# Attention on one core: prologue and first step in one order, first keys in two loads, next operands on GpSimd's queue

## The chip, the cores and the metric

The kernel runs on one core of one Trainium2 chip. The metric is the device time of the whole program in microseconds. Before the change it is 2620.65 us, the median of 3 runs (2619.8 to 2622.64). The engines are PE (TensorE, matmuls), DVE (VectorE), ACT (ScalarE), POOL (GpSimd) and SP (SyncE, which only issues DMAs here). All times in the traces count from the start of the program's first instruction.

## What is computed

The reference is two layers on 2 x 2048 tokens of width 256. The first is a linear recurrence beside a sign-weight projection. The second, to which this case belongs, is an attention with linear position biases, beside a block with its own attention and a mixture of eight experts. The two attentions of the second layer are computed by one function of the kernel:

```python
# first attention: 16 heads of 16, biases by distance
scores = einsum('bhqd,bhkd->bhqk', Q, K) / sqrt(hd) + slopes[:, None, None] * rel
attn   = softmax(where(rel <= 0, scores, -inf))
out    = einsum('bhqk,bhkd->bqhd', attn, V)
# second attention: 16 query heads on 4 key heads, rotary positions, causal
scores = einsum('bqhd,bkhd->bhqk', apply_rope(q), apply_rope(k)) * scale
probs  = softmax(where(causal, scores, min))
attn   = einsum('bhqk,bkhd->bqhd', probs, v)
```

## The kernel before

The program runs in stages: front, middle, attention, after, experts. The change is in the attention (`attention`, from line 974) and in the functions that make its order (from line 896).

The attention has 16 steps (`STEPS`). A step is one batch and a group of four heads; steps 0 to 7 are the first attention, 8 to 15 the second. A step has five kinds of work:

- **max**: the scores of 128 queries against up to 512 keys for two heads, two matmuls that use one half of the array's rows each (line 1214), with masks on the diagonal (four short matmuls, line 1203). DVE reduces each of the two results to row maxima (line 1410). A step has 80 such pairs: 8 of query block 0, 16 of block 1, 24 of block 2, 32 of block 3.
- **rows**: when a block of 512 queries has all its maxima, DVE joins them (line 1417), POOL splits them into a high and a low part (`parts`, lines 1166 and 1168), PE transposes these (line 1241), ACT copies the rows out (line 1356), and SP stores them into two rows of the query operand (line 1105), so that the next matmul subtracts the maximum. 4 a step.
- **score**: the transposed scores of 128 keys against 512 queries for two heads (line 1229), and two exponentials on ACT (line 1366). 80 pairs a step.
- **value**: the product of four heads' exponentials with the values (line 1329), a group of 8 matmuls in the trace. 40 a step.
- **turn**: the output of a query block, copied by ACT (line 1390), turned by PE (line 1338), divided by DVE (lines 1437 and 1441) and stored by SP (line 1135). 4 a step.

The order of this work is written out by hand: the string `ORDER` has one letter for each (m, r, s, v, t), and every engine goes through it and takes its own share. A step's string begins at max 50 (`LEAD`), rows 3 (`AHEAD`) and score 5 (`SLEAD`): it does the last 30 maxima of its own step and the first 50 of the next. Results of max, score, rows and turn go into a ring of seven PSUM banks (`RING`); `slot_table` gives each its place, and `free_slots` lets PE wait until the bank's last user is done.

Before step 0 stands a prologue of its own on each engine. `orders` builds its list, `BEFORE`: the 50 maxima, with a rows five maxima behind the last one of its block, then the 5 scores. PE waits for all of the step's keys (`s_k`, line 1281) before the first max of block 1; until then it reads 512 keys from `k0a`, which an earlier stage has written. At its end PE waits for all of its maxima, rows and exponentials (lines 1289 to 1291).

The DMA queues: SP loads all keys of step 0 (lines 1110 to 1118, six DMAs of 256 KB and two of 96 KB), its values (line 1119), then stores the prologue's three rows, and then loads the operands of step 1 (lines 1122 and 1123; nine pieces in `LOADS`, two DMAs each but for the last). POOL loads the operands of step t + 2 during step t (line 1183), and puts fills of zeros for a later stage between them (line 1157).

Of the kernel before, what the change touches and what calls it, by code (L numbers as in the profile page):

```python
# [8 lines left out]
F32 = mybir.dt.float32  # L9
# [4 lines left out]
P = 128  # L14
B, L, D = 2, 2048, 256
# [910 lines left out]
NGR = NSP // PAIRS  # L926
LAST_MAX = [max(m for m in range(NMX) if MAXES[m][0] == qb) for qb in range(NQB)]
# [9 lines left out]

def orders():

    kinds = {"m": "max", "r": "rows", "s": "score", "v": "value", "t": "turn"}
    count = {"m": LEAD, "r": AHEAD, "s": SLEAD, "v": 0, "t": 0}
    work = []
    for k in ORDER:
        work.append((kinds[k], count[k]))
        count[k] += 1  # L950
    first = []
    for m in range(LEAD):
        first.append(("max", m))
        first += [("rows", qb) for qb in range(AHEAD) if min(LAST_MAX[qb] + 5, LEAD - 1) == m]
    first += [("score", s) for s in range(SLEAD)]
    whole = {"max": NMX, "rows": NQB, "score": NSP, "value": NGR, "turn": NQB}
    last = [(what, k) for what, k in work if k < whole[what]]
    return first, work, last
# [15 lines left out]
def attention(nc, A, M):  # L974
# [4 lines left out]
    with ExitStack() as ctx:  # L979
# [25 lines left out]
        s_k = sem("att_first_keys_loaded")  # L1005
# [18 lines left out]
        BEFORE, WORK, LAST = orders()  # L1024
        HELD = slot_table(WORK)[1]
        HELD += [("pad", 0)] * (-len(HELD) % RING)
# [17 lines left out]
        def work_of(t):  # L1044
            return LAST if t == STEPS - 1 else WORK
# [48 lines left out]

        block = ctx.enter_context(nc.Block())

        @block.sync
        def _(sp):
# [11 lines left out]
            for j in range(2):  # L1110
                for n in range(NPROD):
                    at = HALF * j + n * HD
                    sp.dma_start(k_op[0][at:at + HD, :, :].bitcast(F32),
                                 M["ka_d"][PROD_K[n], 0:GH * HD, :].rearrange(
                                     "(p j d) t -> j d p t", p=PAIRS, j=2)[j]).then_inc(s_k, 16)
                at = HALF * j + DOTS
                sp.dma_start(k_op[0][at:at + SLOPED + 2, :, :].bitcast(F32),
                             M["aug_d"][SLOPED:2 * SLOPED + 2, j * PAIRS:(j + 1) * PAIRS, :]).then_inc(s_k, 16)
            load(sp, 0, ("values", 0, 0))
            for n in range(AHEAD):  # L1120
                rows(0, n)
            for piece in LOADS:
                load(sp, 1, piece)
# [20 lines left out]
        def _(pool):  # L1144
# [25 lines left out]
            for n in range(AHEAD):  # L1170
                parts(0, n)
            for i in range(STEPS * FILLS, HSROWS // P // FILL):
                empty_rows(i)

            def step(t):
                for what, n in work_of(t):
                    if what == "rows":
                        parts(t, n)
                    elif what == "score" and (n - SLEAD) % LOAD_EVERY == 1 and (
# [12 lines left out]
        def _(pe):  # L1192
# [14 lines left out]
            def max_pair(r, n, outs, keys=None):  # L1207
# [4 lines left out]
                for j in range(2):  # L1212
                    part = slice(HALF * j, HALF * j + max_row(r))
                    ins = pe.matmul(outs[j][:, 0:w], q_op[o][part, p, qt * P:(qt + 1) * P],  # L1214
                                    (keys or k_op[o])[part, kp, k0:k0 + w], start=True, stop=not diagonal)
# [5 lines left out]
            def score_pair(r, n, outs):  # L1221
# [5 lines left out]
                for j in range(2):  # L1227
                    part = slice(HALF * j, HALF * j + max_row(r) + 2)
                    ins = pe.matmul(outs[j][:, c0:QB], k_op[o][part, kp, kt * P:(kt + 1) * P],  # L1229
# [14 lines left out]
            def free_slots(t, held, first, count):  # L1244

                last = {}
                for u in range(first - RING, first - RING + count):
                    past = u < 0
                    what, n = HELD[u] if past else held[u]
                    while what == "pad":  # L1250
                        u -= RING
                        what, n = HELD[u]
# [12 lines left out]
            first_at, first_held = slot_table(BEFORE)  # L1265
            for what, n in BEFORE:
                u = first_at[what, n]
                past = first_held[max(0, u - RING):max(0, u - RING + (1 if what == "rows" else 2))]
                done = [k + 1 + MD0 for kind, k in past if kind == "max"]
                taken = [k + 1 + RE0 for kind, k in past if kind == "rows"]  # L1270
                if done:
                    pe.wait_ge(s_md, max(done))
                if taken:
                    pe.wait_ge(s_re, max(taken))
                exped = [k + 1 + EX0 for kind, k in past if kind == "score"]
                if exped:
                    pe.wait_ge(s_ex, max(exped))
                if what == "max":
                    if n == LAST_MAX[0] + 1:

                        pe.wait_ge(s_k, (2 * NPROD + 2) * 16)
                    max_pair(0, n, [ps[(u + j) % RING] for j in range(2)], M["k0a"] if n <= LAST_MAX[0] else None)
                elif what == "score":
                    if n == 0:
                        pe.wait_ge(s_mr[0], NMR)
                    score_pair(0, n, [ps[(u + j) % RING] for j in range(2)])
                else:
                    turn_rows(0, n, u % RING)
            pe.wait_ge(s_md, 2 * LEAD + MD0)
            pe.wait_ge(s_re, AHEAD + RE0)  # L1290
            pe.wait_ge(s_ex, 2 * SLEAD + EX0)

            def step(t):
# [3 lines left out]
                for what, n in work:  # L1297
# [3 lines left out]
                    if what == "max":  # L1301
                        if n == NMX:
# [968 lines left out]
```

## Time and profile before

| | us |
|---|---|
| median of 3 runs | 2620.65 (2619.8 to 2622.64) |
| profiled execution | 2615.48 |
| its span, first to last instruction | 2613.6 |
| busy in the span: PE, DVE, ACT, POOL | 2339.5, 1918.1, 1515.9, 577.7 |

The span is what the profile sees of the profiled execution; the rest of its time lies around it. Busy times are of the whole program, which goes through stages with different limits, so that they say little about one of them. The attention is the middle part, from some 383 us on to 2010 us. Its stretches are read from views that are cut by time.

### The profile page before, as it was taken

Reading aid. Unit: us, or ns where it says so; the run is one execution under the profiler, and the core shown is the slowest. Engines: PE = TensorE matmul, PEld = TensorE weight load, DVE = VectorE, ACT = ScalarE, POOL = GpSimd, SP = SyncE. Lnnn points to the kernel's source line nnn. Section 1 sums busy time; section 2 is a strip of 40 time slices with the busy share of each in tenths; the row PEclk is TensorE's granted clock in tenths of the full one; section 3 lists DMA queues with packets and bytes.
Section 4 is the critical chain, followed back from the end, with each engine's and each line's share of the span. In section 5 each row is a group of like instructions: output and inputs, shape, how many; then the busy total and the mean of one; then the engine's idle time right before and its main releaser. Section 6 shows DMA issues by size and latency. Waiting matters only on the chain. (4 is left out here: it accounts for less than half of the span.)

```text
span 2613.6 us, 52877 instructions
## 1 busy us (share of the span) xinstructions
PE 2339.5 (90%) x18274; PEld 1272.9 (49%) x18275; DVE 1918.1 (73%) x4030; ACT 1515.9 (58%) x3290; POOL 577.7 (22%) x836
## 2 busy tenths in 40 slices
PE   3299986999999999999999999999997882899997
PEld 2155542444444444444444444444442652788886
DVE  6767666899999999999999999999991563233332
ACT  2033321787787787787787787777776551222221
POOL 4412100111111111111111111111000265523323
PEclk9599995899999999999999999999998995999999
DMA  4157673933433433322322322322102884344443
GB/s 153 60 169 213 203 198 54 134 74 74 79 75 72 81 75 71 68 53 48 68 53 48 69 53 47 69 53 46 33 30 87 280 271 166 78 76 77 76 77 69
DMA packets 169670, 246.99 MB, mean 94 GB/s; under 512 B 52196, under 2 KB 127092, under 8 KB 163408
## 3 DMA queue, kind: packets, MB, share of 16 engines
q0 software_dynamic: 37328, 107.98, 22.2%
q1 hardware_dynamic: 127136, 127.58, 17.6%
q10 hardware_dynamic: 4992, 8.55, 0.9%
q8 instruction: 138, 2.26, 0.4%
q14 instruction: 76, 0.62, 0.1%
HBM read 120.63 MB, written 122.36 MB: 93 GB/s over the span
## 5 line engine op out<-in xcount | busy, mean ns | idle before, releaser
L1410 DVE TENSOR_REDUCE a_mx<-banks 128x1 f32<-128x512 f32 (+3 forms) x2560 | 1379.8, 604 | 150.0 <-PE banks L1214 78.8
L1366 ACT ACTIVATE a_p<-banks 128x512 f32<-128x512 f32 (+3 forms) x2560 | 1177.3, 541 | 317.7 <-PE banks L1229 196.5
L1329 PE MATMUL banks<-a_p,a_v 128*32 128x512 f32 (+3 forms) x5120 | 599.8, 543 | 1.0 <-ACT a_p L1366 0.6
L1214 PE MATMUL banks<-a_k,a_q 48*128 48x512 f32 (+7 forms) x1600 | 340.3, 428 | 8.7 <-DVE a_mx L1410 1.9
L1229 PE MATMUL banks<-a_q,a_k 50*128 50x512 f32 (+7 forms) x1600 | 332.2, 426 | 11.3 <-ACT a_p L1366 4.6
L1214 PEld LDWEIGHTS banks<-a_k,a_q 52*128 52x128 f32 (+1 forms) x1600 | 155.0, 184 | 207.3 <-DVE a_mx L1410 165.9
L1229 PEld LDWEIGHTS banks<-a_q,a_k 54*128 54x128 f32 (+1 forms) x1600 | 152.4, 184 | 199.9 <-DVE a_mx L1410 144.9
L1214 PE MATMUL banks<-a_k,q 52*128 52x512 f32 (+7 forms) x944 | 215.3, 459 | 27.2 <-DMA a_k<-aug_rows 14.2
L1229 PE MATMUL banks<-q,a_k 54*128 54x512 f32 (+3 forms) x960 | 202.1, 434 | 10.4 <-ACT a_p L1366 6.0
L2048 ACT ACTIVATE e_hT<-banks 128x256 fp32r<-128x256 f32 x72 | 27.6, 383 | 311.6 <-PE banks L1976 311.6
L1989 PE MATMUL banks<-w,e_hT 128*128 x576 | 184.5, 422 | 9.4 <-DVE e_hT L2088 9.4
L1214 PEld LDWEIGHTS banks<-a_k,q 48*128 48x128 f32 (+1 forms) x944 | 96.6, 196 | 146.7 <-DVE a_mx L1410 109.1
L1950 POOL DMA_INDIRECT out_rows<-e_y,e_token x72 | 111.5, 1549 | 254.2 <-DVE e_y L2108 165.9
L2088 DVE TENSOR_TENSOR e_hT<-banks,e_hT 128x256 fp32r<-128x256 f32 x72 | 30.6, 424 | 174.7 <-ACT e_hT L2048 174.7
L1329 PEld LDWEIGHTS banks<-a_p,a_v 128*32 128x32 f32 x5120 | 102.9, 108 | 113.4 <-issue 64.1
L1229 PEld LDWEIGHTS banks<-q,a_k 54*128 54x128 f32 (+1 forms) x960 | 92.4, 188 | 132.8 <-DVE a_mx L1410 79.9
L2008 PE MATMUL banks<-w,e_gT 128*128 x576 | 136.6, 380 | 1.4 <-DVE e_y L2108 1.1
L1989 PEld LDWEIGHTS banks<-w,e_hT 128*128 128x128 f32 x576 | 110.1, 192 | 33.6 <-issue 10.7
L1203 PE MATMUL banks<-fill,before 64*128 64x64 bf16 x2048 | 125.9, 199 | 0.0
L1203 PE MATMUL banks<-fill,after 64*128 64x64 bf16 x2048 | 121.9, 197 | 0.0
L2008 PEld LDWEIGHTS banks<-w,e_gT 128*128 128x128 f32 x576 | 104.0, 191 | 13.3 <-issue 2.3
L1157 POOL DMA_DIRECT2D expert_rows<-a_zeros x132 | 98.8, 748 | 2.8 <-issue 2.8
(257 smaller groups left out, 2465.9 us busy)
## 6 DMA issues: line engine op xcount, KB each, us to landing
expert_rows<-a_zeros POOLq DMA_DIRECT2D x132, 258.0 KB, 5.4
e_x<-expert_rows SPq DMA_DIRECT2D x72, 129.0 KB, 3.0
a_k<-ka_parts POOLq DMA_DIRECT2D x36, 256.0 KB, 6.4
expert_rows<-e_y SPq DMA_DIRECT2D x72, 128.0 KB, 2.2
qa_parts<-m_part SPq DMA_DIRECT2D x16, 512.0 KB, 4.7
ka_parts<-m_part SPq DMA_DIRECT2D x16, 512.0 KB, 5.1
va_tiles<-m_va SPq DMA_DIRECT2D x8, 1024.0 KB, 5.3
qb_parts<-m_part SPq DMA_DIRECT2D x16, 512.0 KB, 4.7
```

The source lines that it names most:

```text
L1157: pool.dma_start(hs[:, i * FILL:(i + 1) * FILL, :], zeros[:, :, :]).then_inc(s_zs, 16)
L1203: ins = pe.matmul(outs[j][:, HALF * n:HALF * (n + 1)], steps[n][half, :], fill[half, :], start=False, stop=(n == 1))
L1214: ins = pe.matmul(outs[j][:, 0:w], q_op[o][part, p, qt * P:(qt + 1) * P], (keys or k_op[o])[part, kp, k0:k0 + w], start=True, stop=not dia ...
L1229: ins = pe.matmul(outs[j][:, c0:QB], k_op[o][part, kp, kt * P:(kt + 1) * P], q_op[o][part, p, qb * QB + c0:(qb + 1) * QB], start=True, sto ...
L1329: ins = pe.matmul(ps_o[VW * h:VW * h + VW, c0:QB], v_op[o][:, kt, hk * VW:hk * VW + VW], prob[:, (n * GH + h) % NPB, c0:QB], start=(kt == ...
L1366: nc.scalar.activation(prob[:, (2 * n + j) % NPB, c0:QB], ps[(slot + j) % RING][:, c0:QB], ACT.Exp, scale=SCALE).then_inc(s_ex, 1)
L1410: v.tensor_reduce(mx[:, j, p, qt, k0 // WIDE:k0 // WIDE + 1], ps[banks[j]][:, 0:w], AX.X, ALU.max).then_inc(s_md, 1)
L1950: pool.indirect_dma_start(out=out, out_offset=bass.IndirectOffsetOnAxis(ap=token[n % R][:, :], axis=0), in_=y[n % R][:, :], in_offset=None ...
L1989: ins = pe.matmul(bank[:, :], hT[c][s][:, k, :], of[:, ds(e * KD + k, 1), part * FFN:(part + 1) * FFN].rearrange("p o m -> p (o m)"), star ...
L2008: ins = pe.matmul(ps_y[:, 0:D], gT[s][:, f, :], w2[:, ds(e * FT + f, 1), :].rearrange("p o m -> p (o m)"), start=(f == 0), stop=(f == FT - 1))
L2048: nc.scalar.activation(hT[0][s][:, :, :].rearrange("p k t -> p (k t)"), ps_h[:, 0:D], ACT.Copy).then_inc(s_hi, 1)
L2088: v.tensor_tensor(hT[1][s][:, :, :].rearrange("p k t -> p (k t)"), ps_h[:, 0:D], high, ALU.subtract).then_inc(s_hT, 1)
```

## The change

The prologue and step 0 become one list. A new string, `FIRST_ORDER`, gives it entry by entry: 130 maxima (the 80 of step 0 and the first 50 of step 1), 85 scores, 40 value products, 7 rows and 4 turns. The loops over `BEFORE` on PE, ACT and DVE and PE's waits at the prologue's end are gone, and step 0 takes the new list (`work_of`). The first rows stands behind the eighth max. Keys below 512 are read from `k0a` throughout step 0 (`keys_of`), by the scores too.

The keys of step 0 from 512 to 1023 are loaded by SP, those from 1024 to 2047 by ACT, which loads the values behind them; each part has a semaphore, and PE waits for the first at max 9 and for the second at max 26 (`KEYED`). The operands of step 1 are issued by POOL, a piece at max 20, 25, ... 60, each when PE has scored that many; those of step 2 at score 26, 33, ... 82. Four fills of zeros move from before step 0 to the start of step 1.

```diff
+KEYED = [min(m for m in range(NMX) if MAXES[m][3] >= k0) for k0 in (WIDE, 2 * WIDE)]
...
+FIRST_ORDER = (
+    "mmmmmmmmrmmmmmmmmmsmmsmmsmsmmsvmmmmrvmmsmmmsmsmmsmvvsmmmvsmsmsmmvsmsmmmsvsmsmsvmsmrtsmms"
+    "vmmvsmmsvvmsmsmmsvsmsmmvsmsmvsmmsmsmvsmsmmsmvsmsmmssvmmsvmmsmsmmrmsmmvsmsvmmmsvmmvssmmvs"
+    "msvmmsmmvsmrmsmsvssmmvmsmmsvmsmsmvsmsmsmrvsmsmvsmsvmsmsvstsmsvmsmsmvsmsmvsssmmvsmsvvmsst"
+    "tr"
+)
...
+    first = numbered(FIRST_ORDER, {"m": 0, "r": 0, "s": 0, "v": 0, "t": 0})
+    work = numbered(ORDER, {"m": LEAD, "r": AHEAD, "s": SLEAD, "v": 0, "t": 0})
...
-            return LAST if t == STEPS - 1 else WORK
+            return FIRST if t == 0 else LAST if t == STEPS - 1 else WORK
...
+        def first_step_keys(eng, done, lo, hi):
+
+            for j in range(2):
+                for n in range(NPROD):
+                    at = HALF * j + n * HD
+                    eng.dma_start(k_op[0][at:at + HD, :, lo:hi].bitcast(F32),
+                                  M["ka_d"][PROD_K[n], 0:GH * HD, lo:hi].rearrange(
+                                      "(p j d) t -> j d p t", p=PAIRS, j=2)[j]).then_inc(done, 16)
...
-            load(sp, 0, ("values", 0, 0))
-            for n in range(AHEAD):
-                rows(0, n)
-            for piece in LOADS:
-                load(sp, 1, piece)
+            first_step_keys(sp, s_k[0], BT, 2 * BT)
...
-            for n in range(AHEAD):
-                parts(0, n)
-            for i in range(STEPS * FILLS, HSROWS // P // FILL):
-                empty_rows(i)
-
             def step(t):
+                if t == 1:
+                    for i in range(STEPS * FILLS, HSROWS // P // FILL):
+                        empty_rows(i)
                 for what, n in work_of(t):
                     if what == "rows":
                         parts(t, n)
-                    elif what == "score" and (n - SLEAD) % LOAD_EVERY == 1 and (
+                    elif t == 0 and what == "max" and n % 5 == 0 and 0 <= n // 5 - 4 < len(LOADS):
+                        pool.wait_ge(s_mt, n)
+                        load(pool, 1, LOADS[n // 5 - 4])
+                    elif t == 0 and what == "score" and n % 7 == 5 and 0 <= n // 7 - 3 < len(LOADS):
+                        pool.wait_ge(s_sc, n)
+                        load(pool, 2, LOADS[n // 7 - 3])
+                    elif t > 0 and what == "score" and (n - SLEAD) % LOAD_EVERY == 1 and (
...
-            for what, n in BEFORE:
...
-            pe.wait_ge(s_md, 2 * LEAD + MD0)
-            pe.wait_ge(s_re, AHEAD + RE0)
-            pe.wait_ge(s_ex, 2 * SLEAD + EX0)
...
+                        if t == 0 and n == KEYED[0]:
+                            pe.wait_ge(s_k[0], NFK)
+                        if t == 0 and n == KEYED[1]:
+                            pe.wait_ge(s_k[1], NFK)
...
+            first_step_keys(act, s_k[1], 2 * BT, L)
+            load(act, 0, ("values", 0, 0))
```

How the instructions stand: on PE, from the eighth max pair (512 keys from `k0a`) on. Before, the maxima of block 1 follow (keys `a_k`), and the transposes of the first rows (`a_mpart`) stand among them:

```order
L1214 MATMUL banks<-k0a,q 128x512 x2
L1203 MATMUL banks<-fill,before 128x64 x4
L1214 MATMUL banks<-a_k,q 128x512 x2
L1214 MATMUL banks<-a_k,q 128x128 x2
L1203 MATMUL banks<-fill,before 128x64 x4
L1214 MATMUL banks<-a_k,q 128x512 x2
L1214 MATMUL banks<-a_k,q 128x256 x2
L1203 MATMUL banks<-fill,before 128x64 x4
L1214 MATMUL banks<-a_k,q 128x512 x2
L1241 MATMUL banks<-ident,a_mpart 8x128 x4
```

After, from the same pair on (line 1235 is the max, 1262 the transposes):

```order
L1235 MATMUL banks<-k0a,q 128x512 x2
L1220 MATMUL banks<-fill,before 128x64 x4
L1262 MATMUL banks<-ident,a_mpart 8x128 x4
L1235 MATMUL banks<-k0a,q 128x512 x2
L1235 MATMUL banks<-a_k,q 128x128 x2
L1220 MATMUL banks<-fill,before 128x64 x4
L1235 MATMUL banks<-k0a,q 128x512 x2
L1235 MATMUL banks<-a_k,q 128x256 x2
L1220 MATMUL banks<-fill,before 128x64 x4
```

The transposes moved ahead of the maxima of block 1, and the first of these reads `k0a`.

Further on in the same list on PE, after: scores (line 1250) and a value product (1329) stand among the maxima of blocks 1 and 2, where before there were maxima and rows alone up to the fiftieth pair.

```order
L1235 MATMUL banks<-a_k,q 128x384 x2
L1220 MATMUL banks<-fill,before 128x64 x4
L1250 MATMUL banks<-q,k0a 128x384 x2
L1220 MATMUL banks<-fill,after 128x64 x4
L1235 MATMUL banks<-k0a,q 128x512 x2
L1235 MATMUL banks<-a_k,q 128x512 x2
L1220 MATMUL banks<-fill,before 128x64 x4
L1250 MATMUL banks<-q,k0a 128x256 x2
L1220 MATMUL banks<-fill,after 128x64 x4
L1329 MATMUL banks<-a_p,a_v 32x512 x4
```

Scores and values of step 0 moved into the stretch of the first maxima.

On SP at the start of the attention, before: keys, values, the three row stores of the prologue (two DMAs each), then the operands of step 1.

```order
L1113 DMA a_k<-ka_parts 16x2x2048 x3
L1117 DMA a_k<-aug_rows 6x4096
L1113 DMA a_k<-ka_parts 16x2x2048 x3
L1117 DMA a_k<-aug_rows 6x4096
L1092 DMA a_v<-va_tiles 128x16x128
L1105 DMA q<-a_mrow 2x2x512 x6
L1066 DMA a_q<-qa_parts 16x2x2048
```

After, on SP:

```order
L1114 DMA a_k<-ka_parts 16x2x512 x3
L1118 DMA a_k<-aug_rows 6x2x512
L1114 DMA a_k<-ka_parts 16x2x512 x3
L1118 DMA a_k<-aug_rows 6x2x512
L1131 DMA q<-a_mrow 2x2x512 x6
```

SP keeps a quarter of the keys and the row stores. Half of the keys and the values went to ACT, the operands of step 1 to POOL, and the first quarter of the keys is no longer loaded.

## Rows read from the trace of the kernel before

**Rows 1.** Busy time in three stretches; the first line names the columns
```profile
core 0: us, PE busy (x) PEld busy (x) DVE busy (x) ACT busy (x) POOL busy (x), PEclk, DMA share, GB/s
384.10:447.50 63.40, 38.46 (x204) 18.59 (x202) 50.29 (x102) 1.17 (x2) 2.58 (x9) 0.50 0.32 44
447.50:560.80 113.30, 107.70 (x983) 49.41 (x982) 91.67 (x176) 84.39 (x182) 19.79 (x39) 0.89 0.68 113
560.80:658.50 97.70, 95.73 (x935) 43.78 (x930) 89.23 (x173) 77.42 (x168) 17.00 (x34) 1.00 0.42 76
```

**Rows 2.** DVE in order of time: start, duration, instruction, idle before and releaser
```profile
384.11 6.49 DVE L1410 TENSOR_REDUCE a_mx<-banks 128x1 f32<-128x128 f32 x16 [5.82 <-PE banks L1203]
390.71 0.18 DVE L1417 TENSOR_REDUCE a_rowtop<-a_mx 128x16 f32<-128x16 f32 x1
...
403.68 16.03 DVE L1410 TENSOR_REDUCE a_mx<-banks 128x1 f32<-128x512 f32 x32 [12.79 <-PE banks L1214]
...
419.91 25.59 DVE L1410 TENSOR_REDUCE a_mx<-banks 128x1 f32<-128x512 f32 x48
...
455.55 1.29 DVE L1410 TENSOR_REDUCE a_mx<-banks 128x1 f32<-128x512 f32 x2 [7.35 <-PE banks L1214]
```

**Rows 3.** PE's waits from 384.1 to 447.5: total, times, longest (us)
```profile
PE banks L1214 <- DMA a_k<-aug_rows: 14.2, 1, 14.2
PE banks L1214 <- DVE a_mx L1410: 7.4, 18, 0.9
```

**Rows 4.** Busy time by stretches of 10 us, columns as in rows 1
```profile
430.00:440.00 10.00, 7.48 (x32) 3.20 (x32) 10.00 (x20) 0.00 (x0) 0.00 (x0) 0.50 0.00 0
...
460.00:470.00 10.00, 10.00 (x66) 3.91 (x64) 7.77 (x14) 6.35 (x13) 1.00 (x3) 0.50 0.97 121
470.00:480.00 10.00, 9.84 (x94) 4.45 (x91) 8.67 (x15) 6.37 (x15) 0.74 (x1) 0.93 1.04 172
```

**Rows 5.** All engines in order of time, 391 to 407
```profile
391.02 0.19 POOL L1151 COPY a_zeros<-a_numbers 128x2 f32<-128x2 f32 x1 [7.11 <-DMA a_numbers<-in_c_ids]
...
391.59 0.21 POOL L1168 TENSOR_TENSOR a_mpart<-a_rowtop,a_mpart 128x16 fp32r<-128x16 f32 x1
...
402.77 0.90 PE L1214 MATMUL banks<-a_k,q 52*128 52x512 f32 x4 [14.18 <-DMA a_k<-aug_rows]
...
405.94 1.02 PE L1241 MATMUL banks<-ident,a_mpart 128*8 128x128 f32 x4
```

**Rows 6.** DMAs issued from 382 to 404: KB each, median us to landing
```profile
a_k<-ka_parts SPq DMA_DIRECT2D x6, 256.0 KB
a_v<-va_tiles SPq DMA_DIRECT2D x1, 1024.0 KB, 18.9
a_k<-aug_rows SPq DMA_DIRECT2D x2, 96.0 KB
```

**Rows 7.** PE's groups, 454.7 to 470.65: busy us, mean ns | idle
```profile
L1329 PE MATMUL banks<-a_p,a_v 128*32 128x512 f32 (+3 forms) x40 | 7.1, 805 | 0.0
L1214 PE MATMUL banks<-a_k,q 52*128 52x512 f32 (+2 forms) x18 | 6.1, 670 | 0.0
L1229 PE MATMUL banks<-q,a_k 54*128 54x512 f32 (+2 forms) x18 | 5.3, 617 | 2.1 <-ACT a_p L1366 2.1
```

**Rows 8.** PE in order of time in a steady step, upper clock
```profile
702.09 1.06 PE L1329 MATMUL banks<-a_p,a_v 128*32 128x512 f32 x8
703.08 0.50 PE L1229 MATMUL banks<-a_q,a_k 54*128 54x512 f32 x2
```

**Rows 9.** ACT, POOL and SP in order of time, each from its own answer
```profile
449.81 4.15 ACT L1366 ACTIVATE a_p<-banks 128x512 f32<-128x512 f32 x10
...
455.51 0.52 POOL L1066 DMA_DIRECT2D a_q<-qa_parts  x1 [6.25 <-PE banks L1203]
...
560.76 0.40 SPq L1135 DMA_DIRECT2D attention_rows<-a_orow  x1
```

**Rows 10.** A group of DMAs issued from 448 to 500, columns as in rows 6
```profile
a_k<-ka_parts POOLq DMA_DIRECT2D x5, 256.0 KB, 16.5
```

## What was predicted

> **What bounds the kernel now.** I read first the busy time by stretch [rows 1]. A steady step of the attention takes 97.7 us, with PE busy for 95.7 and DVE for 89.2: PE sets the pace, DVE is close behind. The 50 max pairs of the prologue (384.1 to 447.5) take 63.4 us, and its 5 scores with step 0 (to 560.8) take 113.3, though step 0 has the same instructions as any other step. Under the prologue's maxima ACT does 1.2 us of work and PE 38.5; in the second stretch ACT does 84. So work for PE and ACT, which could lie under the prologue's maxima, comes after them.
>
> Then the chain of DVE in that stretch [rows 2] and PE's waits [rows 3]. DVE reduces eight pairs in 6.5 us, is idle for 12.8, and then runs without a gap: 16 pairs in 16.0 us, 24 in 25.6, which is 1.07 us a pair. The idle time is PE's wait of 14.2 us for the first keys. Later PE waits 18 times for DVE: the prologue is DVE-bound. Step 0 begins with the reverse, DVE idle for 7.4 us [rows 2] until its next pair comes from PE.
>
> Then the granted clock [rows 4]. In the prologue it is at the lower level (1.2 GHz), with PE busy for 7.5 of 10 us; at 460 to 470 PE is busy throughout and the level is still the lower one; in the next 10 us it reads 0.93, so it rose to 2.4 GHz at about 471.4. PE had had no idle time since 454.7 [rows 7].
>
> **What the changed order costs: the start.** I count from DVE's first reduce (384.1) to the end of step 0, which SP's last store of step 0 marks at 560.8 [rows 9]: 176.7 us. The order string has 266 entries in place of 50 maxima, 3 rows, 5 scores and 208 entries of step 0: the same 130 max pairs, 85 scores, 40 value products, 7 rows, 4 turns. No arithmetic goes or comes; all that changes is what lies beside what.
>
> The first eight pairs stay: DVE is done at 390.9. Now the four transposes of block 0's row maxima stand directly behind them on PE, where they stood five pairs later. That is a new wait: PE holds for GpSimd's two small operations, which end at 391.8 because GpSimd itself waits for its numbers until 391.0; the transposes take 1.0 us, and a first reduce follows its first matmul by 0.9 [rows 5]. Behind PE there DVE waits: it resumes at 391.8 + 1.0 + 0.9 = 393.7, not 403.7. The ninth pair reads keys that are already there (k0a); the tenth needs the new first load. **Its landing** is not shown by the trace. The old one, 1.7 MB on SP, released PE at 402.8, with the values behind it landing 18.9 us after issue; 2.7 MB in all from 384 to 405, about 0.13 MB a us [rows 5, 6]. The first load is a quarter of the keys, 0.42 MB. Alone it takes 3.2 us (387); if ACT's stream gets two bytes for each of its own (its rows are twice as long), 9.6 us (394); behind everything, 403. I take 394, for two queues are filled at the same time; the tenth pair is then hardly late. The rest of the keys is asked for at pair 27, some 18 us later, and all 2.7 MB are in by 405: nothing for that. ACT's nine DMA issues lie where ACT has nothing to do [rows 1]. If the cover on GpSimd fails and the numbers land 4 us later, DVE starts 4 us later.
>
> By the Trainium skill (DMA: Bandwidth & Descriptors, section Issuing engines are not separate DMA queues) DMAs issued by several engines share the same 16 engines and interleave, and issuing from a second one saves only issue time. That speaks against loading on SP and ACT side by side, and by it the later end (403) is possible; no row of before has two bulk loads of this kind, and this rival is priced below from rows.
>
> **The stretch up to entry 145.** Prices of PE. At half clock [rows 7]: 40 value matmuls, five products worth 3.5 full widths, 7.1 us, so 2.03 a full width; the other 8.85 us for 18 pairs, 0.49 a pair with its masks. At full clock: a value product every 0.99 us (702.09 to 703.08) [rows 8]; a step has 34 full widths of them, so its 95.7 us leave 0.388 a pair, rows and turns included. DVE: 1.07 a pair back to back, 89.2 / 80 = 1.115 in a step.
>
> Entries 9 to 47 (28 max pairs, 8 scores, 2 value products worth 1.75 widths, one rows): DVE 16.0 + 12.8 = 28.8, and by the higher price 30; PE at half clock 36 x 0.49 + 1.75 x 2.03 + 1.0 = 22.2. DVE sets it: 393.7 + 30 = 423.7.
> Entries 48 to 81 (16 max, 12 scores, 4.5 widths): DVE 17; PE 28 x 0.49 + 4.5 x 2.03 = 22.9 at half clock, 15.4 at full. Here PE becomes the later one and so has no more gaps; after 17 us of that the clock rose before [rows 4, 7]. I take 20, between 17 and 22.9: 443.7.
> Entries 82 to 144 (28 max, 22 scores, 9.5 widths): DVE 28 x 1.115 = 31.2, PE at full clock 50 x 0.388 + 9.4 = 28.8: 31.2, so 474.9.
>
> **The rest.** Entries 145 to 215 (35 max, 23 scores, 9.75 widths): these maxima are the first 35 of step 1, 8 in 6.5, 16 in 16.0 and 11 at 1.07, 34.3, by the step's price 35.7; PE 32.2. Entries 216 to 265 (15 max, 20 scores, 8.5 widths, three of the four turns, two rows): PE 13.6 + 8.4 = 22, and some 2 more for turns beyond their share: 24; DVE 16.7. Sum 59.7, so 534.6. A steady step loses 2.0 us beside its bound (97.7 - 95.7); with that and a little for the worse fit, 537. **Saved: 560.8 - 537 = 23.8 us**, of which 10 from the keys and the rest from scores, products and exponentials that now lie under the maxima, less the half clock. The floor is DVE: with no gap after 393.7 and 1.07 a pair for 122 pairs, it is done at 524, 36 us saved.
>
> **Queues.** Step 1's operands were issued by SP behind the prologue's three row stores, step 2's by GpSimd; now GpSimd issues both, one piece at each fifth pair from 20 to 60 and at each seventh score from 26 to 82. Each piece is one or two issues of 0.5 us [rows 9], and what stands behind them on GpSimd is the parts of the next rows, so a rows may be late by 1 us; PE stands before it, with up to three reduced pairs of stock for DVE. SP is freed: its row stores have no bulk behind or before them. The last piece needed at pair 80 (entry 145, about 475) is asked for at pair 55 (entry 90, about 448). Such pieces landed after 16.5 us under the heaviest load [rows 10], so 465: 10 us to spare, cost nothing; if landing took 50 us it would cost 23. The four fills of zeros that moved to step 1 are four issues on GpSimd, which is busy for 17 of 97.7 us there [rows 1].
>
> **The sum against the times.** The profiled execution took 2615.5 us, 5.2 below the median of 2620.65. The difference carries over: 2620.65 - 23.8 = 2596.8.
>
> **Rivals.**
> 1. The keys land with everything, at 403. For: two streams on the same engines. Against: the first DMAs are a quarter as long and are issued first. DVE does one more pair, waits until 403.7, loses 8.8: 15 saved, 2605.6. Chance 0.13.
> 2. **The clock stays low.** The mechanism: DVE holds PE in gaps of up to 0.9 us, and at 7.5 busy of 10 the prologue never left the lower level [rows 3, 4]. The place is entries 9 to 144, where I count DVE as the bound. If it stays low to entry 145, entries 48 to 144 take PE 22.9 + 50 x 0.49 + 9.5 x 2.03 + 3 = 70 in place of 51: 5 saved, 2616, chance 0.06. If it stays low to the end of the order, the rest takes 93 x 0.49 + 18.25 x 2.03 + 8 = 91 in place of 60: 26 lost, 2647, **slower**, chance 0.04. It turns to a loss from about 15 us behind entry 145, where the clock would have to be low still at 508. Against it: at half clock PE has 70 us of work from entry 48 to 144 and DVE 48, so PE has no gaps there, and without gaps the clock rose at 471.
> By the Trainium skill (TensorE: Matmul & The Clock Gate, section A second HAM failure mode: psum-queue depth-cycling) a kernel that cycles through PSUM banks, with PE idle for moments between its groups, saw its clock swing between both levels. That is this rival with swings; the steps here, seven banks in a ring, are at full clock throughout, which speaks against it.
> 3. Step 1's operands are late, or the order meshes worse than its sums, by 10: 2607, chance 0.04. That the order does not reach the chip is excluded: PE's instructions stand in the new order.
>
> **How the numbers follow.** The forecast has 0.73. A measurement of this kernel tells about 0.2% from no change, 5.2 us. Faster: 0.73 + 0.13 + 0.04 and a third of the 0.06: 0.92. Same 0.04, slower 0.04. The range: 2588 (33 saved, near the floor of 36) to 2612 (9 saved), which takes in late keys, late operands and a clock that rises some 20 us later than I count; the clock that stays low is left out, as is what lies beyond.
>
> **What would show it.** DVE's idle time after its first eight pairs near 3 us, not 12.8. The clock at its upper level from 430 to 450, before 471. DVE busy for 9 of 10 us from 394 to 510. ACT's exponentials beginning near 406, not 449.8 [rows 9]. The last store of step 0 at 537; steps of 97.7 after it. I am wrong if PE still waits for the first keys at 400, if the clock is low at 475, or if PE waits for a load at pair 80.

## The result, and the profile after

The changed kernel takes 2598.83 us in the median (2594.56 to 2600.93, 4 runs) against 2620.23 before (the three runs that stand above and a fourth): 21.4 us less. The quotient of the medians is 0.9918; the estimate of the ratio from all runs is 0.9913, 95% interval 0.9897 to 0.9929. Timed again beside a later run it was 0.9908 (0.9894 to 0.9922). The forecast was 2596.8, with 2588 to 2612 as its range. The profiled execution took 2600.93, the slowest of the four; its span is 2599.1.

The stretch counted in the prediction, from DVE's first reduce to SP's last store of step 0, was 176.7 us [rows 2, 9]. It is now 383.62 to 539.49, which is 155.9: 20.8 saved where 23.8 were forecast. By the first reduce of the next step's string, against which the last store now stands 1.2 earlier, it is 19.6. From then on a step takes 97.8 (638.46 to 736.24), as before. SP in order of time (start, duration, instruction):

```profile
539.49 0.85 SPq L1148 DMA_DIRECT2D attention_rows<-a_orow  x1
...
638.46 0.40 SPq L1148 DMA_DIRECT2D attention_rows<-a_orow  x1
...
736.24 0.39 SPq L1148 DMA_DIRECT2D attention_rows<-a_orow  x1
```

The spans of the two profiled executions differ by less than that, 14.5 us (2613.6 and 2599.1). The clock falls at the end of the attention at 2010.8 before and at 1992.9 now, 17.9 earlier, and the stages behind it, which the change does not touch, took 602.8 and 606.2. The difference lies in the last of them (columns as in rows 1; first the kernel before, then the changed one):

```profile
2250.00:2613.60 363.60, 347.89 (x1750) 295.14 (x1748) 122.70 (x336) 91.59 (x201) 110.34 (x72) 0.98 0.42 75
```
```profile
2232.10:2599.10 367.00, 351.00 (x1756) 296.84 (x1754) 122.78 (x338) 91.66 (x201) 110.38 (x72) 0.98 0.41 75
```

Over the twelve profiles of this document the stages behind the attention take 599.9 to 606.2 us. So a single execution's total says little about gains of a few us, and a stretch of it says more.

DVE in order of time at the start (start, duration, instruction, idle before and releaser), which answers to [rows 2]:

```profile
383.62 6.50 DVE L1406 TENSOR_REDUCE a_mx<-banks 128x1 f32<-128x128 f32 x16 [5.81 <-PE banks L1220]
390.22 0.18 DVE L1413 TENSOR_REDUCE a_rowtop<-a_mx 128x16 f32<-128x16 f32 x1
393.05 1.29 DVE L1406 TENSOR_REDUCE a_mx<-banks 128x1 f32<-128x512 f32 x2 [2.65 <-PE banks L1235]
395.13 15.32 DVE L1406 TENSOR_REDUCE a_mx<-banks 128x1 f32<-128x128 f32 x30 [0.79 <-PE banks L1220]
```

The idle time of 12.79 us has become 2.65 and 0.79. Who is waited for is seen in the order of time of PE, POOL and ACT:

```profile
391.20 1.01 PE L1262 MATMUL banks<-ident,a_mpart 128*8 128x128 f32 x4 [3.09 <-POOL a_mpart L1181]
...
394.48 0.47 PE L1235 MATMUL banks<-a_k,q 52*128 52x128 f32 x2 [1.54 <-DMA a_k<-aug_rows]
...
390.84 0.21 POOL L1181 TENSOR_TENSOR a_mpart<-a_rowtop,a_mpart 128x16 fp32r<-128x16 f32 x1
...
401.55 1.28 ACT L1366 ACT_TABLE_LOAD   x1 [8.71 <-PE banks L1220]
402.84 1.09 ACT L1366 ACTIVATE a_p<-banks 128x512 f32<-128x512 f32 x2
```

The first wait is for POOL's parts of the first rows, the second for the first keys. The first exponential begins at 402.8, where it began at 449.8 [rows 9]. Busy time by stretches of 10 us (columns as in rows 1), against [rows 4]:

```profile
430.00:440.00 10.00, 9.80 (x76) 4.52 (x72) 7.56 (x15) 5.71 (x12) 0.99 (x2) 0.68 0.54 82
440.00:450.00 10.00, 8.26 (x76) 3.94 (x76) 9.24 (x19) 6.42 (x14) 2.26 (x5) 1.00 0.50 85
450.00:460.00 10.00, 9.51 (x74) 3.84 (x72) 8.83 (x17) 5.24 (x13) 4.02 (x6) 0.85 0.37 105
460.00:470.00 10.00, 9.43 (x84) 3.97 (x82) 10.00 (x19) 7.10 (x15) 1.74 (x3) 0.98 0.76 130
```

The clock rises at 436.4, where it rose at 471.4, and falls back once, from 456.9 to 460.3. PE and DVE are both busy for 7.5 to 10 of every 10 us, and DVE for 106.7 of the 116 us from 394 to 510; in [rows 4] it was first DVE alone that was full, and then PE alone.

### The profile page after: what moved, and what is told of

Read it like the earlier page. It is cut to its first block and busy times, and to the rows that moved or that the text cites. A ratio compares the mean times of both kernels' runs of the same rounds, so it can differ in the third digit from the quotient of the medians.

```text
span 2599.1 us, 52888 instructions
## 1 busy us (share of the span) xinstructions
PE 2340.3 (90%) x18274; PEld 1272.7 (49%) x18275; DVE 1918.0 (74%) x4030; ACT 1517.6 (58%) x3290; POOL 590.2 (23%) x853
## 5 line engine op out<-in xcount | busy, mean ns | idle before, releaser
L1250 PE MATMUL banks<-a_q,a_k 50*128 50x512 f32 (+7 forms) x1600 | 332.2, 426 | 11.5 <-ACT a_p L1366 4.4
L1235 PE MATMUL banks<-a_k,q 48*128 48x512 f32 (+7 forms) x896 | 193.6, 437 | 6.8 <-DMA a_k<-aug_rows 1.5
L1250 PE MATMUL banks<-q,a_k 50*128 50x512 f32 (+7 forms) x896 | 187.0, 429 | 6.9 <-ACT a_p L1366 2.9
L1235 PEld LDWEIGHTS banks<-a_k,q 48*128 48x128 f32 (+1 forms) x896 | 89.1, 190 | 116.1 <-DVE a_mx L1406 92.0
L1250 PEld LDWEIGHTS banks<-q,a_k 50*128 50x128 f32 (+1 forms) x896 | 84.9, 185 | 122.7 <-DVE a_mx L1406 77.3
L1998 PEld LDWEIGHTS banks<-w,e_gT 128*128 128x128 f32 x576 | 103.8, 190 | 13.5 <-issue 2.3
```

The source lines that it names most:

```text
L1250: ins = pe.matmul(outs[j][:, c0:QB], keys_of(r, kt * P)[part, kp, kt * P:(kt + 1) * P], q_op[o][part, p, qb * QB + c0:(qb + 1) * QB], star ...
L1998: ins = pe.matmul(ps_y[:, 0:D], gT[s][:, f, :], w2[:, ds(e * FT + f, 1), :].rearrange("p o m -> p (o m)"), start=(f == 0), stop=(f == FT - 1))
```

## The experiments

The table has, for each kernel, the time from DVE's first reduce to the start of some later max pairs (pair 36 is entry 48 of the order, 52 entry 82, 80 entry 145; pair 130 is the first of the next step's string), all from DVE's order of time in one profiled execution each; the two of the changed kernel differ by up to 1.9 us. The last column is the median of the timed runs and its ratio to the kernel before on the same chip.

| kernel | pair 9 | 36 | 52 | 80 | 130 | time, ratio (95%) |
|---|---|---|---|---|---|---|
| before | 20.8 | 48.6 | 76.1 | 113.8 | 175.5 | 2620.23 |
| the change | 11.5 | 41.9 | 63.8 | 97.0 | 155.9 | 2598.83, 0.9913 (0.9897 to 0.9929) |
| keys alone | 13.3 | 41.2 | 68.0 | 106.2 | 174.1 | 2613.16, 0.9982 (0.9973 to 0.9992) |
| without the keys | 19.0 | 48.3 | 68.4 | 100.5 | 159.3 | 2600.55, 0.9934 (0.9918 to 0.9951) |
| without POOL's queue | 13.2 | 42.3 | 60.6 | 109.5 | 170.8 | 2612.83, 0.9980 (0.9971 to 0.9990) |
| 17 matmuls more | 13.6 | 48.0 | 67.0 | 99.1 | 158.0 | 2600.34, 0.9939 (0.9922 to 0.9956) |
| keys on one queue | 10.6 | 39.4 | 61.0 | 93.1 | 151.9 | 2593.84, 0.9904 (0.9888 to 0.9921) |
| and rows later | 7.9 | 38.7 | 60.6 | 92.7 | 151.6 | 2592.37, 0.9898 (0.9880 to 0.9916) |
| without the order | 13.5 | 41.5 | 67.4 | 102.3 | 163.2 | 2607.08, 0.9955 (0.9940 to 0.9970) |
| pairs twice | 13.2 | 44.2 | 65.3 | 98.7 | 157.5 | 2600.17, 0.9924 (0.9905 to 0.9942) |
| block 0 denser | 7.9 | 41.2 | 61.1 | 93.2 | 152.0 | 2592.55, 0.9899 (0.9884 to 0.9913) |
| the change again | 13.4 | 42.4 | 64.0 | 96.1 | 154.9 | 2595.41, 0.9908 (0.9894 to 0.9922) |

My theory going in was that of the prediction: 10 us from the keys, the rest from scores and values under the maxima, nothing from the queues. Its rivals were that the order alone gives the whole gain, and that the clock takes some of it back.

### The keys alone

To the kernel before only the new key loads, with the two waits and the use of `k0a` that go with them. The loads, cut:

```diff
-            for j in range(2):
-                for n in range(NPROD):
-                    ...
-            load(sp, 0, ("values", 0, 0))
+            first_step_keys(sp, s_k[0], BT, 2 * BT)
...
+            first_step_keys(act, s_k[1], 2 * BT, L)
+            load(act, 0, ("values", 0, 0))
```

> The kernel before with the keys alone changed: first keys (512 to 1023) on SP, the rest and the values on ACT, keys below 512 from k0a; prologue and step 0 keep their order. My theory, the two parts of the change add up: PE gets the tenth pair's keys at about 394.4 as in the changed kernel, DVE's idle time falls from 12.8 us to 3 or 4 (the ninth pair is done at once, for the rows stand five pairs later here), everything behind moves up by 9.5 us: last store of step 0 near 551, time about 2611. Rival, the order gives the whole gain and an earlier prologue is lost again at the start of step 0 (clock, table load, waits for exponentials): 2620.

Measured: 0.9982, some 5 us, between the two. The keys do what they should: pair 36 comes 7.4 us earlier than before, and pair 52 is 8.1 earlier. Then most of it is lost in the profiled execution (1.4 are left at pair 130), and PE's order of time tells where:

```profile
491.30 0.47 PE L1224 MATMUL banks<-a_k,a_q 52*128 52x128 f32 x2 [4.74 <-DMA a_k<-aug_rows]
```

That is pair 80, the first that reads step 1's operands. SP issues them behind the third row store, as before, while pair 80 is reached earlier: they are late. The clock falls 1.5 us before that wait ends, at 489.8, and stays low until 506.9, with PE full behind the wait (busy time by stretches, columns as in rows 1; the clock is the number behind the busy times):

```profile
489.90:506.80 16.90, 15.50 (x106) 7.77 (x108) 7.69 (x19) 5.47 (x12) 2.18 (x5) 0.50 0.88 116
```

So a wait of 4.7 us was followed by 15.6 us at 1.2 GHz: from pair 80 to pair 100 this kernel takes 28.7 us, the one before 22.5. The theory of two parts that add up had left the queue out.

### The change without the keys

```diff
-            first_step_keys(sp, s_k[0], BT, 2 * BT)
+            first_step_keys(sp, s_k[0], 0, L)
+            load(sp, 0, ("values", 0, 0))
...
-            first_step_keys(act, s_k[1], 2 * BT, L)
-            load(act, 0, ("values", 0, 0))
...
-                        if t == 0 and n == KEYED[1]:
-                            pe.wait_ge(s_k[1], NFK)
```

> The changed kernel with the order alone: all keys of step 0 and behind them the values on SP in one load, as before. My theory: PE is held at the tenth pair until about 402.3 in place of 394.5, DVE loses 8 us there, and nothing later gives them back, since behind it one of DVE and PE is always the bound: last store of step 0 near 548, time about 2607. Rival, the order hides the load (the later part is bound by PE at the upper clock, and the clock rises at its own time): 2599 to 2601.

PE is held as expected, and DVE with it (pair 9 at 19.0 in place of 11.5):

```profile
403.51 0.48 PE L1236 MATMUL banks<-a_k,q 52*128 52x128 f32 x2 [8.88 <-DMA a_k<-aug_rows]
```

But of these 7.5 us only 3.4 are left at pair 130; they are made up between pair 26 and pair 80. Against the second profile of the change (last row of the table) 5.6 are lost at pair 9 and 4.4 are left, so how much comes back differs from one execution to the next. The ratios say 5.5 to 6.8 us (0.9934 against 0.9913 and 0.9908), and as each is known to about 0.0016, the difference is known to about 6 us. In this run the clock rises at 420.8 for 7 us and for good at 437.9, 52.7 us behind the first reduce; with the keys in two loads it is 52.8. By then 40 pairs had been reduced here and 44 there, so fewer were left to the lower level, which would explain it but is not shown. The median of 2600.55 lies in the rival's range; set against the kernel before on the same chip (2618.09, where the expectations count from 2620.65) it lies between theory and rival. The run decides for neither.

### The change without POOL's queue

Step 1's operands go back to SP, behind its third row store:

```diff
                     if what == "rows":
                         rows(t, n)
+                        if t == 0 and n == AHEAD - 1:
+                            for piece in LOADS:
+                                load(sp, 1, piece)
...
-                    elif t == 0 and what == "max" and n % 5 == 0 and 0 <= n // 5 - 4 < len(LOADS):
-                        pool.wait_ge(s_mt, n)
-                        load(pool, 1, LOADS[n // 5 - 4])
```

> The changed kernel with step 1's operands on SP again, issued in one go behind the third row store (about 448), step 2's on GpSimd as in the change. Theory, the queue is worth nothing by itself as long as the operands are there at pair 80 (about 480): 2599. Rival, issued at 448 beside GpSimd's own stream the 3.3 MB of keys and queries need 25 to 50 us: PE waits at pair 80 for up to 20 us, time 2600 to 2619, and GpSimd's queue is what makes the order possible.

The rival is right: 0.9980. PE waits at pair 80 for 15.75 us; the clock falls 4.4 us into that wait, at 481.3, and rises 9.1 us behind it, at 501.8. PE's order of time, and two stretches before and in the wait (columns as in rows 1):

```profile
492.70 0.48 PE L1235 MATMUL banks<-a_k,a_q 52*128 52x128 f32 x2 [15.75 <-DMA a_k<-aug_rows]
...
461.80:477.60 15.80, 14.16 (x120) 5.86 (x112) 15.53 (x29) 10.46 (x23) 2.74 (x5) 1.00 1.02 140
477.60:493.40 15.80, 0.70 (x8) 0.69 (x8) 0.22 (x1) 0.00 (x0) 0.44 (x2) 0.62 1.05 134
```

The next to last number, the DMA engines' share, is 1 throughout: they were busy all the time. PE is released 47.4 us after SP's first issue of these operands (445.3); with the keys alone it was 47.3 (444.0). In the kernel before PE comes to pair 80 47.0 us after that issue (449.6) and does not wait: the burst had been just in time. Its last part, the values, took longer still (from the view of [rows 10]):

```profile
a_v<-va_tiles SPq DMA_DIRECT2D x1, 1024.0 KB, 50.7
```

This run also gives a bound for what the half clock costs, for its PE instructions are those of the change up to pair 52, and its clock rose at 426.7:

```profile
426.20:444.50 18.30, 16.59 (x154) 8.02 (x146) 17.91 (x36) 11.56 (x25) 0.44 (x2) 0.99 0.01 2
```

The changed kernel, in the same entries 48 to 81:

```profile
425.50:447.40 21.90, 20.22 (x154) 9.30 (x146) 18.24 (x37) 11.88 (x25) 4.27 (x9) 0.75 0.59 89
```

At the upper level DVE is busy for 17.9 of 18.3 us, at the mixed level for 18.2 of 21.9: 3.6 us. POOL's issues and their transfers also lie in the second stretch (DMA share 0.59 against 0.01), so that the half clock costs 3.6 at most.

### More matmuls against the clock

Two attempts to bring the clock up earlier. The first adds 17 matmuls on all 128 rows, ten where PE waits and seven between later pairs, the second does the matmuls of the max pairs 8 to 35 twice:

```diff
+                        if t == 0:
+                            for _ in range({7: 7, 8: 3}.get(n, 1 if n in range(10, 23, 2) else 0)):
+                                pe.matmul(ps_o[:, 0:P], ident[:, :], ident[:, :], start=True, stop=True)
```

```diff
+                for j in range(2) if r == 0 and 8 <= n <= 35 else ():
+                    part = slice(HALF * j, HALF * j + max_row(r))
+                    pe.matmul(outs[j][:, 0:w], q_op[o][part, p, qt * P:(qt + 1) * P],
+                              keys_of(r, k0)[part, kp, k0:k0 + w], start=True, stop=True)
```

> The changed kernel with 17 matmuls more on PE, 128 rows by 128 columns, results unused: 7 behind the eighth pair, where PE waits for GpSimd, 3 behind the ninth, where it waits for keys, one behind every second pair from 10 to 22. Theory, the half clock costs the changed kernel the 4 to 5 us that it was late by at entry 82 (447.4 against 443.7) and some at the short fall of the clock near 457: with the clock up by 405 the pairs 36 to 52 take 17 to 18 us in place of 21.8, last store of step 0 near 535, time about 2594. Rival, DVE and the ring set that stretch at either level, or the clock does not rise from this: 2599, or 1 to 3 more for the matmuls in the way.

> The changed kernel in which PE does the matmuls of the max pairs 8 to 35 of step 0 twice, into the same bank; DVE reduces once. 28 pairs more are 13.7 us of PE at half clock (22 + 14 = 36 against DVE's 30) and 9.6 at full. Theory, gaps on PE hold the clock low: with PE full the clock rises by about 412 and stays, entries 48 to 81 take 18.3 us as in the run with step 1's operands on SP, where the clock rose early, in place of 21.8, and the doubled work costs 2 to 4 in its own stretch: 2597 to 2600, with the two visible apart in the trace. Rival, max pairs (48 to 54 of 128 rows in use) do not raise the clock whatever the gaps: the doubled stretch takes 36 us, the clock rises later than 436, 2604 or more.

Neither gains (0.9939 and 0.9924): the first comes out as its rival said; the second has the time that its theory named, but not for its reason, since the clock did not stay up and entries 48 to 81 took 21.1 us in place of 18.3. The clock moves, but does not stay. With the 17 matmuls it is up from 393.1 to 396.5 and for 3.4 us at 424, and for good from 434.0; the matmuls themselves cost 4 us up to pair 36 (34.4 us from pair 9 on, where the change takes 30.4). With the pairs done twice it changes level five times up to 437.0, where it rises, and falls once more from 460.9 to 464.3 (columns as in rows 1):

```profile
399.00:409.00 10.00, 9.12 (x74) 6.21 (x72) 9.00 (x19) 2.37 (x3) 0.00 (x0) 0.63 0.11 33
409.00:419.00 10.00, 9.80 (x82) 5.98 (x78) 7.88 (x16) 3.50 (x8) 2.26 (x6) 0.66 0.42 61
419.00:429.00 10.00, 8.18 (x76) 4.93 (x78) 9.88 (x20) 2.14 (x7) 1.93 (x5) 0.89 0.76 101
429.00:439.00 10.00, 9.71 (x66) 4.34 (x66) 7.51 (x16) 5.20 (x11) 2.04 (x4) 0.60 0.87 131
```

When it is up, PE is done sooner and waits for DVE (8.2 busy of 10); then it falls, and PE is full again (9.7). The clock rises at 406.3 with max pairs and scores alone on PE, so the second rival falls; but while DVE is the later one the level does not hold in these two runs. As a proof that an earlier clock would pay, both runs are inconclusive. What stays open is whether it can be held up in that stretch at all.

### The keys on one queue, and the rows later

```diff
             first_step_keys(sp, s_k[0], BT, 2 * BT)
+            first_step_keys(sp, s_k[1], 2 * BT, L)
+            load(sp, 0, ("values", 0, 0))
...
-            first_step_keys(act, s_k[1], 2 * BT, L)
-            load(act, 0, ("values", 0, 0))
```

> The changed kernel with all loads of step 0 on SP, the first keys (512 to 1023), then the other keys, then the values; nothing on ACT. Theory, SP and ACT share the DMA engines, and the first load is late by that: with its 0.42 MB ahead of everything it lands by 389, PE does not wait for it at the tenth pair (1.5 us in the changed kernel, 3 to 9 in the runs so far), DVE's idle time there falls from 3.4 us to 2.7, which is GpSimd's part alone. Of these 0.8 us perhaps half arrive at the end, for half of the keys' gain was given back in the run with the order alone: 2598, not to be told from the change. Rival, the landing is set by the start of a DMA and not by sharing: PE still waits until 394.

In the second kernel in addition:

```diff
-    "mmmmmmmmrmmmmmmmmmsmm...
+    "mmmmmmmmmmrmmmmmmmsmm...
```

> The kernel with all loads of step 0 on SP, and the first rows two pairs later in the order, behind the tenth max in place of the eighth. Theory, the 2.65 us in which DVE is idle behind its first eight pairs are PE's wait for GpSimd's parts: with two pairs ahead of it and the keys there, DVE runs without a gap from its first reduce, 3.4 us earlier at the eleventh pair than in the changed kernel; 1.5 to 3.4 us of that arrive: 2596 to 2597. Rival, the first scores then wait for the stored rows (seven pairs are left between), or the clock takes it back: 2599.

With one queue PE does not wait for the first keys; DVE's order of time shows the rows' wait alone, and then 23 reduces without a gap:

```profile
393.93 11.35 DVE L1406 TENSOR_REDUCE a_mx<-banks 128x1 f32<-128x512 f32 x23 [2.65 <-PE banks L1237]
```

With two queues the same wait of PE was 1.5 us in the first profile of the change and 3.5 in the second, 2.6 to 3.2 in three of the variants, and 7.5 and 7.8 in the two where PE comes to it earlier. In all seven it ended 12.1 to 14.2 us after SP's first issue. In the second kernel here PE uses the same keys 6.2 us after SP's first issue (383.13), without a wait:

```profile
383.13 1.26 SPq L1114 DMA_DIRECT2D a_k<-ka_parts  x3
```
```profile
389.33 0.47 PE L1237 MATMUL banks<-a_k,q 52*128 52x128 f32 x2
```

So with ACT's loads issued beside it SP's first load lands at least 6 to 8 us later. With the rows two pairs later the wait for POOL is covered too, and the first gap is 0.97 us, two pairs on:

```profile
391.06 1.68 DVE L1406 TENSOR_REDUCE a_mx<-banks 128x1 f32<-128x512 f32 x4
393.71 9.26 DVE L1406 TENSOR_REDUCE a_mx<-banks 128x1 f32<-128x512 f32 x18 [0.97 <-PE banks L1237]
```

PE now waits 1.0 us for the stored rows at the first score, as the rival said, which costs less than it saves. The medians are 2593.84 and 2592.37. Their intervals overlap with those of the change (0.9904 and 0.9898 against 0.9913 and 0.9908), so that 1 to 4 us are likely and not shown; in the profiled executions they are 4.0 and 4.3 us at pair 130 against the first profile of the change, and 3.0 and 3.3 against the second.

### Without the order

The changed kernel with the old order written into the new string:

```diff
-    "mmmmmmmmrmmmmmmmmmsmmsmmsmsmmsvmmmmrvmmsmmmsmsmmsmvvsmmmvsmsmsmmvsmsmmmsvsmsmsvmsmrtsmms"
+    "mmmmmmmmmmmmmrmmmmmmmmmmmmmmmmrmmmmmmmmmmmmmmmmmmmmmrsssssmvsmsssmvms...
```

> The changed kernel with the order of before in the new string: 50 maxima with their three rows, 5 scores, then the string of step 0. Keys in two loads, step 1's operands on GpSimd, one list and no drain at the prologue's end stay. Theory, the drain and the loops are worth next to nothing and the order of scores and values among the maxima is what is left of the gain: as the run with the keys alone, 2611 to 2614. Rival, the drain (PE's 2.9 us of waits for exponentials at the start of step 0) or SP's free queue carry a part: 2605 to 2609.

0.9955, 12 us less than before and 11 more than the change; it lies in the rival's range, 2605 to 2609. Against the run with the keys alone it has POOL's queue for step 1's operands and no drain: no wait at pair 80, no fall of the clock behind it, and 6 to 7 us less. In the profiled executions 7.0 of the 10.9 us between these two at pair 130 arise behind pair 80. So the new order of scores and values, beside the other two parts, is worth about 11 of the 21 us, known to about 6.

### Block 0 denser, and the change again

```diff
-    "mmmmmmmmmmrmmmmmmmsmmsmmsmsmmsvmmmmrvmmsmmmsmsmmsmvvs...
+    "mmmmmmmmmmrmmmmmmmsmmsmsmsmvsmsmmvsmsmmrvmmvmmmmmmsms...
```

> The kernel with the keys on SP and the first rows later, and in it the scores and value products of block 0 closer together: all eight scores stand ahead of the second rows (five before), the four value products end at entry 44 in place of 51. Theory, with the clock low PE is the later one from entry 48 on and has gaps before; work moved forward there (three scores, 2 of 4 value products, 3 us of PE) fills gaps and may let the clock rise before 50 us from the first reduce: pair 52 at 57 to 59 us from the first reduce in place of 60.6, time 1 to 3 us under the run with the rows later. Rival, the gaps on PE are DVE's and ring's, the stretch only gets its wait elsewhere: no difference, 60 to 61.

> The changed kernel once more, on one chip with the run above, so that the two can be set side by side: 0.9913 of the kernel before, as measured. A second profile of it also tells whether the short fall of the clock 73 to 77 us behind the first reduce belongs to the kernel or to one execution, and whether the first keys land 10 to 14 us after their first issue each time.

No difference: 2592.55, pair 52 at 61.1. The clock is up for good 46.3 us from the first reduce in place of 49.8, but pair 36 comes 2.5 later, nearly all of it by pair 26 (30.7 against 28.3): more work of PE stands there at the lower level, and PE waits 2.4 us in place of 1.0 for the stored rows. The rival is right; this one rearrangement gives nothing more. It beats the change by about as much as the two runs before it, within the same uncertainty.

The change again takes 2595.41. Its clock does not fall behind pair 61 as in the first profile, but rises behind pair 24 and falls behind pair 30 once before it rises for good; its first keys land 14.0 us after SP's first issue, 12.1 in the first profile. Both belong to the execution, not to the kernel.

## Why the prediction was right, point by point

**What bounds the kernel** held: DVE sets the first entries, both are full from entry 82 on. **The start** was forecast to within a microsecond: DVE resumes 9.4 us after its first reduce (9.6), PE gets the tenth pair's keys at 394.5 (394). For the keys that is partly luck: 394 was taken between 387 and 403 for a share of two to one that no row showed, and 12.1 us from SP's first issue is the shortest of the seven profiles with two queues; in the others it is 13.6 to 14.2. The new wait for POOL's parts is there with 3.1 us. The rival in which the keys land with everything did not come; the runs on one queue show that it is true in part, since there PE does not wait for them and here it waits 1.5 to 3.5 us.

**Entries 9 to 47** took 32.5 us from pair 8 to pair 36 where I counted 30: 0.8 from the keys, the rest from gaps of PE at half clock, which I had covered with DVE's higher price of 1.115 only in part. **Entries 48 to 81**: 21.9 for 20; the clock rose at 436.4, inside the 430 to 450 that I named. **Entries 82 to 144**: 33.2 for 31.2, 32.1 in the second profile without the fall of the clock. **Entries 145 to 215**: 36.5 for 35.7. **The last 50** with the loss: 22.4 for 26.4. Together 155.9 for 152.9: four stretches came out 7.2 longer, the last one 4.0 shorter, so that the sum is nearer than its terms. The rival of a low clock came in a small form: 3.6 us at most in entries 48 to 81 and one short fall.

**Two terms were put in the wrong place**, though their sum was near. I gave 10 us to the keys; taking them away costs 5.5 to 6.8 by the ratios and 3.4 to 4.4 at pair 130, for a part of what is lost at the start is made up by pair 80. And I gave nothing to POOL's queue, by costing only what it adds. That was right as a cost, and wrong as a share: with the operands on SP the change loses 15 us at pair 130, and the keys alone lose most of their gain to the same wait. I had the sentence for it (if landing took 50 us it would cost 23) but held it against the new queue and not the old one: the 47 us that SP's burst had before pair 80 in the old order shrink to 31.6 in the new, and it needs 47. The view that I took 16.5 us from had 50.7 for the end of that burst. What each part is worth beside the other two is some 6 us for the keys, 11 for the order, 17 for the queue (from the ratios 0.9934, 0.9955 and 0.9980 against 0.9913, each to about 5 or 6 us, so that the keys' share stands only just apart from nothing); they add up to more than the 21, since each needs the others.

By the Trainium skill (DMA: Bandwidth & Descriptors, section Issuing engines are not separate DMA queues) loads from two engines share the same 16 DMA engines; the runs agree, with no wait for the first keys on one queue and 1.5 to 3.5 us on two. Two bulk streams did stand side by side in the kernel before, SP's burst and POOL's pieces behind 449.6 [rows 9, 10], so that this could have been read there. By the Trainium skill (TensorE: Matmul & The Clock Gate, section A second HAM failure mode: psum-queue depth-cycling) PE's moments without work between its groups made the clock of a kernel swing. Here it swings while DVE is the later one, with five changes of level up to 437.0 in the run with the pairs done twice, and not in the steady steps, where PE is.

## What to carry to other kernels

When a step is made earlier, ask of each of its inputs when it was asked for and how long it had: a load that took 47 us and had just that can be the next wait. A wait on PE can cost more than itself: behind the two at pair 80 seen here the clock was low for 15.6 and 9.1 us, and pairs 80 to 100 took 6.2 and 2.5 us longer than in the kernels without that wait. Of loads that are needed one after the other, issue the first ones alone on one queue; a second engine's stream takes their share. Where two engines are within 10% of each other, sum a merged order by stretches with the later of the two in each, at the clock that PE will have there, not by the whole.

## What the runs showed of the hardware

Behind a wait of PE of 4.7 us the clock stayed low for 15.6 us, though PE was busy throughout; behind one of 15.8 us for 9.1. In the first 80 us of the merged order the level differs from one execution of the same kernel to the next (up at 436.4 and down from 456.9 to 460.3 in one, up from 415.0 to 421.8 and for good at 438.9 in the other). The times of this kernel spread over 6.4 and 5.6 us, but the stages behind the attention alone differ by as much. A DMA of 16 KB, POOL's numbers, for which POOL waited 7.1 us in the kernel before [rows 5], landed 6.1 us after its issue in the changed kernel and 3.6 in the one with the keys on one queue; in the seven profiles with two queues it is 5.8 to 6.6, in the three with one 3.6 to 3.7 (DMAs of these two by issue: KB each, us to landing):

```profile
a_numbers<-in_c_ids POOLq DMA_DIRECT2D x1, 16.0 KB, 6.1
```
```profile
a_numbers<-in_c_ids POOLq DMA_DIRECT2D x1, 16.0 KB, 3.6
```
